# Both column groups of a pair of token tiles by seven block products, cut at 354 and 244 columns

## The chip, the cores and the metric

The kernel runs on one core of one Trainium2 chip. The metric is the device time of one execution in microseconds (us); lower is better. PE is TensorE, DVE VectorE, ACT ScalarE, POOL GpSimd, SP the engine that issues most DMAs.

## The reference

32x64 token vectors x of 1024 values pass two linear layers with low-rank experts, and x is added at the end:

```
base = x @ W.T;  logits = x @ Wr.T + 5 * one_hot(language)      # 8 experts of rank 16, top 2
y    = base + 2 * sum_e gate_e * (x @ A_e.T) @ B_e.T
out  = x + y @ Wf.T + b + 2 * sum_e softmax(y @ Wrf.T)_e * (y @ Af_e.T) @ Bm_e   # 4 experts of rank 8
```

All matrices are float32, W and Wf are 1024x1024.

## The kernel before

The kernel never forms y. It makes the fused matrix C = W.T @ [Wf.T | Wrf.T | Af.T] once (stage F, to 100 us), adds the identity to its first 1024 columns for the residual, and then multiplies the tokens by C. Every float32 product is three matmuls on rounded parts, high*high, high*low and low*high, so that one block of 128 depths is three matmuls, each with a weight load of its own. ACT rounds a value to its high part, DVE subtracts to get the low part (`low_part`, L665).

Tokens come in 16 tiles of 128 rows, taken as 8 **pairs** (`pair(j)`). In a pair the columns of C fall in two groups:

- **wide**, 2 x 384 columns (`WIDE = 3 * P`): the first two times 384 columns of z (the part of C that makes the output). The 2x2 blocks (tile 0 or 1; depths 0-511 or 512-1023; first or second 384 columns) are multiplied in the seven-product form instead of eight. P1, P2 and P4 take x itself (`of_x`), P3, P5, P6 and P7 sums of blocks of x (S1 to S4, `of_s`); the right sides are blocks of C (B11, B21, B22) or their differences T1 to T4. One product is 4 depths x 3 = 12 matmuls of 384 columns, so a pair has 84. Partial sums that two outputs share are read from PSUM in between: P1 by ACT (`r1_read`), P6, P7 and P5 by DVE (`u2_read`, `u3_read`, `r22_read`), and PE goes on accumulating in the same bank after that.
- **tail**, 428 columns (`TAIL`): the last 256 of z, 36 of the second layer's logits and projections, and 136 of the first layer's expert projections and logits (`gate_proj`). It is plain: 8 depths x 3 x 2 tiles = 48 matmuls of 428 columns per pair (`tail`), done first, since the gates hang on it.

After the tail DVE and ACT make the gates: logits, top two, exp, and the gated projections u (L958 to L981). PE turns u by two transposes (L1242), and ACT and DVE round and split it. `lora` multiplies it by c0 (three matmuls of 384 columns onto each of four banks, and of 292 for each tile's tail). Then follow the second softmax (`neg_max`, `y_exp`, v), its 32x32 transposes on DVE, and `mixed` (98 rows, 384 or 256 columns). The order of PE in a pair after the first is P1, P6, transposes, P2, lora of the tails, P7, lora, P5, lora, P4, mixed of the tails, lora, three mixed, P3, lora, mixed. The order on every engine is written by hand, and an engine's instructions run in that order. One instruction that waits holds all behind it.

The next pair's tokens are loaded by SP into `stage` when the two low parts of the pair before are made (`x_split`, L665); DVE then makes S1 to S4 (L668, L772, `add_s`), ACT rounds them, DVE splits them at the start of the next pair. Results are added up in `rows` (L995, L1026, L1035, L1043, L1046, L1049) and stored once per pair, 2 x 512 KB; the last pair stores piece by piece. Pair 0 is written apart (it overlaps the end of stage F), the loop runs pairs 1 to 7, on ACT and DVE to 6 with the last apart.

Of the kernel before, what the change touches and what calls it, by code (L numbers as in the profile page):

```python
# [5 lines left out]
def adaln_ffn_kernel(nc, part_2, part_1, part_3, part_4, tokens, gate_proj, mix_rows, language, out):  # L6

# [10 lines left out]
    F32 = mybir.dt.float32  # L18
# [7 lines left out]
    P = 128  # L26
# [17 lines left out]
    WIDE = 3 * P  # L44
    HB = part_4.shape[2]
    HTAIL = HB - WIDE
# [3 lines left out]
    Z_SECOND = P + SMALL2  # L50
    PROJ2_AT = P
    LOGIT2_AT = P + ER2
    TAIL_M = 2 * HTAIL
    PROJ_AT = TAIL_M
    LOGIT_AT = PROJ_AT + ER1
    TAIL = TAIL_M + ER1 + E1

# [13 lines left out]

    BANK_A, BANK_B, BANK_C, BANK_D, BANK_T, BANK_U, BANK_WARM = 3, 0, 1, 2, 4, 6, 7
# [6 lines left out]
    with ctx:  # L80
# [7 lines left out]
        c0_high = sb("c0_high", [P, MCOLS], F32R)  # L88
        c0_low = sb("c0_low", [P, MCOLS], F32R)
        ct_high = sb("ct_high", [P, KC, TAIL], F32R)  # L90
        ct_low = sb("ct_low", [P, KC, TAIL], F32R)
        mix = sb("mix", [MIX, D], F32R)

        c_plain = sb("c_plain", [P, 4, HALF, HB])
# [18 lines left out]
        u = sb("u", [P, 2, ER1])  # L113
        ut_high = sb("ut_high", [P, 2, P], F32R)
        ut_low = sb("ut_low", [P, 2, P], F32R)
# [5 lines left out]
        v = sb("v", [P, 2, ER2])  # L121
# [41 lines left out]
        sb("unused", [P, HALF * (2 * IN_W + 2 * ROWS_A + HB) - 4 * KC * P - 6 * HALF * WIDE - 4 * HALF * P])  # L163
# [5 lines left out]
        block_pair(T4, "t4", t_high, t_low)  # L169

# [26 lines left out]
        vt_plain = c_plain[0:ER2, C12, 0, 0:2 * P].rearrange("p (t c) -> p t c", t=2)  # L197
# [59 lines left out]

# [54 lines left out]
        def both(a, b):  # L312

            return sums[:, BANK_T:BANK_T + 2, a:b]

        def z_tail(t):

            return sums[:, BANK_T + t, 0:2 * Z_SECOND].rearrange("p (a c) -> p a c", c=Z_SECOND)[:, :, 0:P]

        def z_tails():
            return both(0, 2 * Z_SECOND).rearrange("p t (a c) -> p t a c", c=Z_SECOND)[:, :, :, 0:P]

# [37 lines left out]
        def tail_part(t, c):  # L361
            h = HALF if c in (C21, C22) else 0
            a = HTAIL if c in (C12, C22) else 0
            return t[:, h:h + HALF, a:a + HTAIL]

# [3 lines left out]
        def _(sp):  # L369
# [37 lines left out]
            def store_last(j):  # L407

                def block_out(t, a, b):
                    return sp.dma_start(out[(2 * j + t) * P:(2 * j + t + 1) * P, a:b], rows[:, t, a:b])  # L410
# [16 lines left out]
            with sp.Fori(0, PAIRS - 2) as j:  # L427
                load_pair(j + 2)
                store(j)
# [915 lines left out]
```

## Time and profile before

| | |
|---|---|
| three runs | 330.17, 330.62, 330.80 us, median 330.62 |
| the profiled execution | 331.02 us |
| its span, first to last instruction | 329.2 us |
| granted TensorE clock | 1.00 (2.4 GHz) |
| busy | PE 324.2 (98%), PEld 319.4 (97%), DVE 222.3 (68%), ACT 122.2 (37%), POOL 1.4 us |
| bytes | HBM read 18.42 MB, written 8.39 MB |

PE is the matmul row, PEld the weight loads that run beside it. Matmuls overlap (one lasts longer than the time to the start of the next), so a busy share of PE says only that it never stood idle; what a matmul costs is the distance from its start to the next start.

### The profile page before, as it was taken

How to read it: one execution, taken by the hardware profiler on the slowest of the kernel's cores; microseconds unless marked ns; L12 is line 12 of the kernel's file. 1: busy time of each engine (PE TensorE's matmuls, PEld its weight loads, DVE VectorE, ACT ScalarE, POOL GpSimd, SP SyncE). 2: the span in 40 equal slices, each digit the busy share in tenths (PEclk: the TensorE clock that was granted, in tenths of full speed). 3: DMA queues.
4: the chain of work that ended last, by engine and by line, in shares of the span. 5: the costliest groups of instructions: out<-in, count | busy, mean ns of one | idle time of the engine just before them, and what ended most of it. 6: DMA issues, size and time to landing. Idle time of an engine off the chain costs nothing.

```text
span 329.2 us, 5489 instructions
## 1 busy us (share of the span) xinstructions
PE 324.2 (98%) x2039; PEld 319.4 (97%) x2039; DVE 222.3 (68%) x492; ACT 122.2 (37%) x245; POOL 1.4 (0%) x11
## 2 busy tenths in 40 slices
PE   8999999999999999999999999999999999999996
PEld 7999999999999999999999999999999999999995
DVE  3999999998899879258447725834863582485441
ACT  3882836494247235033212513311331350332111
POOL 1000000000000000000000000000000000000000
PEclk9999999999999999999999999999999999999999
DMA  7999000000000303301600600240070033003003
GB/s 243 415 407 278 9 2 0 2 0 2 0 2 0 130 0 99 156 0 28 227 0 0 215 39 0 67 188 0 0 252 3 0 115 139 0 1 127 1 0 127
DMA packets 8188, 26.96 MB, mean 82 GB/s; under 512 B 1038, under 2 KB 2062, under 8 KB 8176
## 3 DMA queue, kind: packets, MB, share of 16 engines
q1 hardware_dynamic: 8032, 26.80, 22.8%
q8 instruction: 7, 0.11, 0.2%
q14 instruction: 5, 0.04, 0.0%
q10 hardware_dynamic: 144, 0.01, 0.0%
HBM read 18.42 MB, written 8.39 MB: 81 GB/s over the span
## 4 chain that ended last, share of the span: by engine, by line
PE 95%; DMA 2%; DVE 1%; SPq 0%; ACT 0%; issue 0%
PE sums L1063 95%; DMA in<-part 2%; PE sums L1242 1%; DVE c_plain L1019 0%; ACT a_high L459 0%; DVE rows L1026 0%; DVE rows L1049 0%; ACT y_exp L626 0%; SPq L374 0%; SPq L376 0%; DVE v L1010 0%; SPq L372 0%; DVE y_half L1007 0%; DVE neg_max L1004 0%; DVE y_scale L1008 0%
## 5 line engine op out<-in xcount | busy, mean ns | idle before, releaser
L1063 PE MATMUL sums<-b_high,a_high 128*128 128x256 f32 (+1 forms) x224 | 45.8, 288 | 0.5 <-ACT a_high L459 0.4
L1063 PE MATMUL sums<-ct_high,st_high 128*128 128x428 f32 x128 | 45.7, 357 | 0.0
L1063 PE MATMUL sums<-ct_high,st_low 128*128 128x428 f32 x128 | 45.7, 357 | 0.0
L1063 PE MATMUL sums<-ct_low,st_high 128*128 128x428 f32 x128 | 45.6, 356 | 0.0
L1063 PE MATMUL sums<-b_high,a_low 128*128 128x256 f32 (+1 forms) x224 | 45.4, 286 | 0.0
L1063 PE MATMUL sums<-b_low,a_high 128*128 128x256 f32 (+1 forms) x224 | 45.3, 285 | 0.0
L1063 PEld LDWEIGHTS sums<-b_high,a_high 128*128 128x128 f32 x224 | 34.9, 190 | 1.3 <-DVE b_high L796 0.5
L1063 PEld LDWEIGHTS sums<-b_high,a_low 128*128 128x128 f32 x224 | 34.9, 189 | 0.0
L1063 PEld LDWEIGHTS sums<-b_low,a_high 128*128 128x128 f32 x224 | 34.8, 189 | 0.0
L1063 PE MATMUL sums<-t_high,s_low 128*128 128x384 f32 x96 | 32.4, 337 | 0.0
L1063 PE MATMUL sums<-t_high,s_high 128*128 128x384 f32 x96 | 32.4, 337 | 0.0
L1063 PE MATMUL sums<-t_low,s_high 128*128 128x384 f32 x96 | 32.4, 337 | 0.0
L958 DVE TENSOR_TENSOR logits<-sums,lang_bias 128x16 f32<-128x16 f32 x8 | 1.4, 173 | 42.7 <-PE sums L1063 42.7
L609 ACT ACTIVATE pair_exp<-top 128x1 f32<-128x1 f32 x16 | 3.8, 287 | 67.8 <-DVE top_at L965 67.8
L459 ACT ACTIVATE rows<-sums 128x384 f32<-128x384 f32 (+1 forms) x24 | 12.6, 524 | 34.6 <-PE sums L1063 34.5
L1063 PEld LDWEIGHTS sums<-ct_high,st_low 128*128 128x128 f32 x128 | 24.1, 188 | 0.8
L1063 PEld LDWEIGHTS sums<-ct_low,st_high 128*128 128x128 f32 x128 | 24.1, 188 | 0.8
L1063 PEld LDWEIGHTS sums<-ct_high,st_high 128*128 128x128 f32 x128 | 24.1, 188 | 0.7
L1063 PE MATMUL sums<-c_high,st_high 128*128 128x384 f32 x64 | 22.4, 349 | 0.0
L1063 PE MATMUL sums<-c_low,st_high 128*128 128x384 f32 x64 | 21.7, 339 | 0.0
L1063 PE MATMUL sums<-c_high,st_low 128*128 128x384 f32 x64 | 21.7, 339 | 0.0
L665 DVE TENSOR_TENSOR st_low<-stage,st_high 128x1024 fp32r<-128x1024 f32 x14 | 17.1, 1225 | 5.7 <-ACT st_high L459 5.4
(132 smaller groups left out, 679.4 us busy)
## 6 DMA issues: line engine op xcount, KB each, us to landing
stage<-tokens SPq DMA_DIRECT2D x14, 512.0 KB, 3.6
out<-rows SPq DMA_DIRECT2D x14, 512.0 KB, 4.2
in<-part SPq DMA_DIRECT2D x7, 585.0 KB, 9.2
in<-part SPq DMA_DIRECT2D x4, 777.0 KB, 14.7
in<-part SPq DMA_DIRECT2D x4, 265.0 KB, 17.6
rows<-tokens SPq DMA_DIRECT2D x2, 512.0 KB, 16.2
out<-rows SPq DMA_DIRECT2D x4, 192.0 KB, 2.1
c_plain<-gate_proj SPq DMA_DIRECT2D x1, 544.0 KB, 17.1
```

What stands on the lines that cost most here:

```text
L459: return nc.scalar.activation(out_, in_, ACT.Copy)
L609: ins = nc.scalar.activation(pair_exp[:, t:t + 1], top[:, t, 0:1], ACT.Exp, bias=top[:, t, 1:2], scale=-1.0)
L665: return nc.vector.tensor_tensor(dst, src, as_f32(high), ALU.subtract)
L958: link(nc.vector.tensor_tensor(logits[:, :, :], both(LOGIT_AT, LOGIT_AT + E1), lang_bias[:, bass.ds(2 * j, 2), :], ALU.add))
L1063: return nc.tensor.matmul(out_, lhs, rhs, start=start, stop=stop, skip_group_check=True)
L1242: last = nc.tensor.transpose(ut_psum[:, t, :], u[:, t, :], ident[:, :])
```

## The change

Columns are regrouped. Halves of C are now the two natural halves of z (512 columns each) with the 18 columns of the second layer behind each. The wide group is the first 354 columns of each half (`WIDE = 354`). Of each half the rest, 158 of z and 18, together with half of the 136 gate columns (68), is a **narrow** group of 244 columns (`NARROW`). Pairs 0 and 1 do the narrow group as the tail was done, by 48 matmuls of 2 x 244 = 488 columns. From pair 2 on it goes by seven block products too (`narrow_products`): 84 matmuls of 244 columns into banks 4, 5 and 6. Four more right sides (`tn_high`, `tn_low`) are made in pair 1, for which the gate columns are loaded once more by four DMAs, 272 bytes a run. The partial sums are read into a new tile `narrow`, by ACT (two reads of 244 columns) and DVE (five additions); after mixed, DVE adds the narrow sums to z's last columns (632 elements; ACT copied 512 before), and a new small addition makes `sec`. S sums, their roundings and splits move to other places in the order.

```diff
-    WIDE = 3 * P
+    WIDE = 354
+    GH = (ER1 + E1) // 2
+    NARROW = GH + HTAIL
-    BANK_A, BANK_B, BANK_C, BANK_D, BANK_T, BANK_U, BANK_WARM = 3, 0, 1, 2, 4, 6, 7
+    BANK_A, BANK_B, BANK_C, BANK_D, BANK_T, BANK_U, BANK_WARM = 3, 0, 1, 2, 4, 7, 7
+    BANK_NA, BANK_NB, BANK_NC = 4, 5, 6
...
 # SP
+            sp.wait_ge(cw_split, 3)
+            sp.wait_ge(t_split, 4)
+            for c in (C11, C12, C22, C21):
+                ...
+                sp.dma_start(c_plain[:, c, :, GATE_AT:WIDE], gate_proj[:, k:k + HALF, a:a + GH])\
+                    .then_inc(gate_again, 16)
...
 # ACT, pair(j)
+                if steady:
+                    act.wait_ge(p1n_done, j - 1)
+                    copy(narrow[:, 1, 0, :], narrow_bank(BANK_NA)).then_inc(r1n_read, 1)
+                    act.wait_ge(p2n_done, j - 1)
+                    copy(narrow[:, 0, 0, :], narrow_bank(BANK_NA)).then_inc(n11_out, 1)
-                act.wait_ge(tails_done, j + 1)
-                copy(rows[:, :, 2 * WIDE:D]..., z_tails()).then_inc(tails_out, 1)
...
 # DVE, pair(j)
-                    for n in (S2, S1, S3, S4):
-                        split_s(j, n)
+                    split_s(j, S1)
+                    split_s(j, S4)
+                if second:
+                    dve.wait_ge(gate_again, 64)
+                    make_tn(C11, C12, C11, t1n_made)
+                    make_tn(C12, C22, C12, t3n_made)
+                    split_tn(T1)
+                    make_tn(C11, C22, C11, t2n_made)
+                    next_s(S1)
+                    split_tn(T3)
...
+                if steady:
+                    link(add_sums(sec_halves, tails(SEC_AT, NARROW), narrow[:, :, :, SEC_AT:NARROW]))
+                else:
+                    link(nc.vector.tensor_copy(sec_halves, tails(SEC_AT, NARROW)))
...
 # PE
+            def narrow_product(n, a_high, a_low, a_at, b_high, b_low, fresh):
+                for k in range(HALF):
+                    for kind in (HH, HL, LH):
+                        lhs = (a_high, a_high, a_low)[kind]
+                        rhs = (b_high, b_low, b_high)[kind]
+                        last = mm(narrow_bank(n), lhs[:, a_at[0], a_at[1] + k, :], rhs[:, k, :],
+                                  start=fresh and k == 0 and kind == HH, stop=k == HALF - 1 and kind == LH)
+                return last
...
             pair(0, first=True)
-            with pe_loop(1, PAIRS) as j:
+            pair(1, second=True)
+            with pe_loop(2, PAIRS) as j:
                 pair(j)
```

PE at the start of a pair in the loop, up to the first wide product. L1063, now L1258, is the helper that issues every matmul; c11 is B11, ct holds the tail's columns of C. Before:

```order
L1218 REGISTER_ALU [waits tails_out]
L1063 MATMUL sums<-ct_high,st_high 128x428 [waits x_split_0]
L1063 MATMUL sums<-ct_low,st_high 128x428
L1063 MATMUL sums<-ct_high,st_low 128x428
...
L1063 MATMUL sums<-ct_high,st_high 128x428 [waits x_split_1]
...
L1063 MATMUL sums<-c11_high,st_high 128x384 [waits a_out]
```

Now, of the products P1, P6, P2, P7, P5, P4 and P3 the first matmul each:

```order
L1258 MATMUL sums<-ct_high,st_high 128x244 [waits x_split_0]
...
L1258 MATMUL sums<-ct_high,s_high 128x244 [waits s_split]
...
L1258 MATMUL sums<-ct_high,st_high 128x244 [waits r1n_read]
...
L1442 REGISTER_ALU [waits u2n_read]
L1258 MATMUL sums<-t_narrow,s_high 128x244 [waits s_split]
...
L1258 MATMUL sums<-t_narrow,s_high 128x244 [waits s_split]
...
L1258 MATMUL sums<-t_narrow,st_high 128x244 [waits u3n_read,x_split_1,tn_split]
...
L1258 MATMUL sums<-ct_high,s_high 128x244 [waits r22n_read,s_split]
...
L1258 MATMUL sums<-c11_high,st_high 128x354 [waits a_out]
```

Beside the waits for operands there are now four for reads of the banks (r1n_read by ACT; u2n_read, u3n_read, r22n_read by DVE), each of the result of the last product but one.

DVE at the start of a pair in the loop, up to the logits. Before:

```order
L665 TENSOR_TENSOR s_low<-s_plain,s_high 128x512 [waits s_rounded]
L756 REGISTER_ALU
L665 TENSOR_TENSOR s_low<-s_plain,s_high 128x512 [waits s_rounded]
L957 REGISTER_ALU
L958 ISA [waits narrow_ready]
L958 TENSOR_TENSOR logits<-sums,lang_bias 128x16
```

Now, after the splits of S1 and S4:

```order
L1039 TENSOR_TENSOR narrow<-sums,narrow 128x244 [waits p6n_done,r1n_read]
L1039 TENSOR_TENSOR narrow<-sums,narrow 128x244 [waits p7n_done]
L866 ISA
L867 ISA [waits s_split]
L869 TENSOR_TENSOR s_plain<-stage 128x512 [waits x_here_1,x_here_0]
L1039 TENSOR_TENSOR narrow<-sums,narrow 128x244 [waits p5n_done,u3n_read]
L871 REGISTER_ALU
L765 TENSOR_TENSOR s_plain<-s_plain,stage 128x512 [waits s1_made]
L1039 TENSOR_TENSOR narrow<-sums,narrow 128x244 [waits p4n_done]
L765 TENSOR_TENSOR s_plain<-stage 128x512
L1039 TENSOR_TENSOR narrow<-sums,narrow 128x244 [waits p3n_done,u2n_read]
```

Three S sums of the next pair (s_plain) stand now between the additions, and the first of them waits for the next pair's tokens (x_here). At the end of a pair the low part of the next pair's second tile (st_low) has moved from before L1043's addition to behind that of L1046.

## Rows read from the trace of the kernel before

**Rows 1.** The page: busy time of each engine, and the granted clock in 40 slices

```profile
PE 324.2 (98%) x2039; PEld 319.4 (97%) x2039; DVE 222.3 (68%) x492; ACT 122.2 (37%) x245; POOL 1.4 (0%) x11
...
PEclk9999999999999999999999999999999999999999
```

**Rows 2.** The chain that ended last: start us, us, engine, what, count

```profile
119.22 0.18 DVE neg_max L1004
...
121.91 0.57 DVE rows L1026
...
199.12 27.92 PE sums L1063 x156
227.04 0.22 PE sums L1242 x2
```

**Rows 3.** Engines in a steady pair: stretch, us, busy us of each (instructions), PEclk, DMA

```profile
213.30:241.44 28.14, 28.14 (x160) 27.80 (x160) 15.82 (x44) 7.86 (x19) 0.00 (x0) 1.00 0.21 75
```

**Rows 4.** Timeline of PE: start us, us, instruction; places where the form changes

```profile
60.28 0.28 PE L1063 MATMUL sums<-b_high,bt_high 128*128 128x256 f32 x1
...
60.64 0.29 PE L1063 MATMUL sums<-b_high,bt_high 128*128 128x274 f32 x1
...
61.02 0.41 PE L1063 MATMUL sums<-b_high,a_high 128*128 128x256 f32 x2
...
201.09 0.30 PE L1063 MATMUL sums<-c_high,ut_high 128*128 128x292 f32 x1
...
201.89 0.34 PE L1063 MATMUL sums<-t_high,s_high 128*128 128x384 f32 x1
...
213.30 0.35 PE L1063 MATMUL sums<-ct_high,st_high 128*128 128x428 f32 x1
...
222.64 0.34 PE L1063 MATMUL sums<-c_high,st_high 128*128 128x384 f32 x1
...
226.88 0.38 PE L1242 MATMUL sums<-ident,u 128*128 128x128 f32 x2
227.02 0.42 PE L1063 MATMUL sums<-c_high,st_high 128*128 128x384 f32 x1
227.28 0.34 PE L1063 MATMUL sums<-c_low,st_high 128*128 128x384 f32 x1
...
232.64 0.34 PE L1063 MATMUL sums<-t_high,s_high 128*128 128x384 f32 x1
...
234.72 0.34 PE L1063 MATMUL sums<-c_high,ut_high 128*128 128x384 f32 x1
```

**Rows 5.** Groups by form, weight loads: xcount, busy us, mean ns of one

```profile
L1063 PEld LDWEIGHTS sums<-ct_high,st_high 128*128 128x128 f32 x128 | 24.1, 188 | 0.7
```

**Rows 6.** Groups by form, DVE: what the added instructions are priced by

```profile
L665 DVE TENSOR_TENSOR s_low<-s_plain,s_high 128x512 fp32r<-128x512 f32 x28 | 17.5, 686 | 1.7 <-ACT s_high L459 1.6
L665 DVE TENSOR_TENSOR ut_low<-sums,ut_high 128x256 fp32r<-128x256 f32 x8 | 3.4, 424 | 0.7 <-ACT ut_high L459 0.7
L747 DVE TENSOR_TENSOR c_plain<-sums,c_plain 128x548 f32<-128x548 f32 x6 | 4.3, 718 | 0.0
L665 DVE TENSOR_TENSOR st_low<-stage,st_high 128x1024 fp32r<-128x1024 f32 x14 | 17.1, 1225 | 5.7 <-ACT st_high L459 5.4
```

**Rows 7.** Timeline of DVE and ACT in a steady pair (last bracket: idle before, releaser)

```profile
212.44 0.55 DVE L1043 TENSOR_TENSOR rows<-sums,rows 128x384 f32<-128x384 f32 x1
212.91 0.55 DVE L1046 TENSOR_TENSOR rows<-sums,rows 128x384 f32<-128x384 f32 x1
...
222.96 0.17 DVE L958 TENSOR_TENSOR logits<-sums,lang_bias 128x16 f32<-128x16 f32 x1 [6.08 <-PE sums L1063]
...
225.02 0.49 ACT L459 ACTIVATE rows<-sums 128x384 f32<-128x384 f32 x1 [0.47 <-PE sums L1063]
...
226.11 0.34 DVE L981 SCALAR_TENSOR_TENSOR u<-sums,pair_scale,gates 128x128 f32<-128x128 f32 x1
```

**Rows 8.** The tile stage: its DMAs' time to landing

```profile
DMA to landing us min/median/max: 3.4/3.6/5.1
```

**Rows 9.** Timeline of PE in pair 0: the wait before P4

```profile
121.96 0.34 PE L1063 MATMUL sums<-c_high,ut_low 128*128 128x384 f32 x1
...
122.61 0.41 PE L1063 MATMUL sums<-t_high,st_high 128*128 128x384 f32 x1 [0.31 <-DVE rows L1026]
```

More of the change, by code:

```diff
@@ L636, in pair @@
                 copy(vt[0:ER2, :, :], vt_plain[0:ER2, :, :]).then_inc(v_rounded, 1)
-                if not first:
-                    act.wait_ge(stored[0], 16 * j)
-                act.wait_ge(tails_done, j + 1)
-                copy(rows[:, :, 2 * WIDE:D].rearrange("p t (a c) -> p t a c", c=P), z_tails()).then_inc(tails_out, 1)
+                if not first and not last:
+                    round_next(j + 1, S3, p7_done)
                 if not last:
@@ L645, in pair @@
                     round_x(j + 1, 1)
+                if not first:
+                    act.wait_ge(stored[0], 16 * j)
                 act.wait_ge(a_done, j + 1)
-                copy(rows[:, 0, 0:WIDE], bank(BANK_A)).then_inc(a_out, 1)
+                copy(rows[:, 0, wide_at(0)], bank(BANK_A)).then_inc(a_out, 1)
+                if first:
+                    round_next(j + 1, S2, p6_done)
+                    round_next(j + 1, S3, p7_done)
+                if not last:
+                    round_next(j + 1, S1, p5_done)
             pair(0, first=True)
-            with act.Fori(1, PAIRS - 1) as j:
+            pair(1, second=True)
+            with act.Fori(2, PAIRS - 1) as j:
                 pair(j)
@@ L911, in _ @@
             split_tail(C12)
-            dve.wait_ge(ident_added, 2)
+            dve.wait_ge(ident_added, 1)
             add_out(Q_P7, C22, 0, C22)
@@ L938, in _, with make_tn, split_tn, add_sums @@
             split_t(T3, C12)
+            def make_tn(dst, a, b, made):
+                minus(narrow_of(dst), narrow_of(a), narrow_of(b)).then_inc(made, 1)
+            def split_tn(n):
+                dve.wait_ge(tn_rounded, TN_ORDER.index(n) + 1)
+                low_part(tn_low[n], narrow_of(C12 if n == T3 else C11), tn_high[n]).then_inc(tn_split, 1)
+            def add_sums(dst, n, onto):
+                return nc.vector.tensor_tensor(dst, n, onto, ALU.add)
             STEPS = 14
             BLOCK = 32
-            def pair(j, first=False, last=False):
+            def pair(j, first=False, second=False, last=False):
+                steady = not first and not second
                 base = STEPS * j + VEC_START
@@ L1030, in pair @@
                 if not last:
                     split_x(j + 1, 0)
[L1033 to L1039 removed]
+                if first:
+                    add_r22()
+                    for n in MADE:
+                        next_s(n)
@@ new lines, in pair @@
+                if second:
+                    split_s(j + 1, S2)
+                if steady and not last:
+                    split_s(j + 1, S3)
+                dve.wait_ge(tails_done, j + 1)
+                if steady:
+                    add_sums(rows_tail, tails(GH, SEC_AT), narrow[:, :, :, GH:SEC_AT]).then_inc(tails_out, 1)
+                else:
+                    nc.vector.tensor_copy(rows_tail, tails(GH, SEC_AT)).then_inc(tails_out, 1)
+                if second:
+                    split_s(j + 1, S3)
@@ L1055, in _ @@
             pair(0, first=True)
-            with dve.Fori(1, PAIRS - 1) as j:
+            pair(1, second=True)
+            with dve.Fori(2, PAIRS - 1) as j:
                 pair(j)
```

471 lines of the change are left out of this document (314 added, 157 removed).

## The prediction

> **What bounds the kernel now.** I read the page's busy shares first: PE 98%, weight loads 97%, DVE 68%, ACT 37%, clock at the upper level (2.4 GHz) in all 40 slices [rows 1]. Then the chain that ended last: from 123 us on it is nothing but matmuls, in steps of 28.14 us (27.92 and 0.22) with no other engine in between [rows 2]. The steady pairs are thus pure matmul time: in one, PE is busy for all 28.14 us and DVE for 15.82 [rows 3]. So the change is worth what it does to the matmuls' own distances, less any wait it brings in. The distances come from the timeline, by dividing the stretch between two changes of form by the matmuls in it [rows 4]:
>
> - 128 columns: two transposes and one wide matmul take 227.28 - 226.88 = 0.40 us; less 0.175 for the wide one leaves 0.11 each
> - 256: (60.64 - 60.28) / 3 = 120 ns
> - 274: (61.02 - 60.64) / 3 = 127 ns
> - 292: (201.89 - 201.09) / 6 = 133.3 ns
> - 384: (226.88 - 222.64) / 24 = 176.7 ns, and (234.72 - 232.64) / 12 = 173.3 ns; I take 175.5
> - 428: (222.64 - 213.30) / 48 = 194.6 ns
>
> A slice of columns costs about 0.46 ns per column at the top, and about 0.38 between 256 and 292.
>
> **The change, part by part.** Measured in columns it gives almost nothing on the narrow side: 48 x 428 = 20,544 before, 84 x 244 = 20,496 after. The eighth product that is saved pays for the 30 columns by which each wide matmul shrinks.
>
> *Wide, every pair.* 84 matmuls go from 384 to 354 columns. Between 292 and 384 a column costs (175.5 - 133.3) / 92 = 0.459 ns, so 30 columns are 13.8 ns and a pair saves 84 x 13.8 = 1.16 us.
>
> *Narrow, pairs 2 to 7.* 48 x 194.6 = 9.34 us go. What 244 columns cost no row shows; the nearest is 256 at 120 ns. From below, 244 in proportion to the 384 row (0.457 ns each) is 111.5 ns; from above, no gain on 256 at all, 120 ns, if the weight load sets the pace. I take the line through 256 and 274, 120 - 12 x 0.39 = 115.3 ns, as the nearest rows lie on it: 84 x 115.3 = 9.69 us, so +0.35 us (bounds +0.03 and +0.74).
>
> A rule speaks against this part. Each matmul here has a weight load of 128 columns, and the two transposes, which move only 128 columns, still stand 0.11 us apart [rows 4]: there the load, not the stream, sets the pace. The Trainium skill (page "TensorE: Matmul & The Clock Gate", section "LDWEIGHTS (loading the stationary operand)") gives a load as columns / 1.2, 107 ns for 128, which the 0.11 bears out, and under its "Back-to-back issue gap" N / 2.4 + 2.5 ns for the stream, 104 ns for 244 columns. By the page a 244-column matmul would be held by its load at 107 ns. With its own figures for 354, 384 and 428 as well (150, 162.5, 180.8) a pair would gain an estimated 1.05 - 0.31 = 0.74 us, close to what I get; but 384 columns measure 175.5 and not 162.5, so the sum goes by the rows.
>
> *Lora and mixed.* 12 lora and 4 mixed matmuls lose 30 columns (-0.22 us), 6 grow from 292 to 352 (+0.165), 2 from 256 to 316 (+0.045): nothing.
>
> **A steady pair** comes to -1.16 + 0.35 = -0.81 us, 27.33 after 28.14; six of them -4.9 us (bounds: 1.13 each, -6.8; 0.42 each, -2.5).
>
> *Pairs 0 and 1* have the longer plain tail: 60 columns more at 194.6 / 428 are 27.3 ns, times 48 is +1.31 us; the wide side gives 1.16 back. +0.15 each, +0.3.
>
> *New waits in the narrow products.* P2, P7, P4 and P3 each wait for a read of a bank, and one other product (12 x 115 ns = 1.38 us) covers it. A reader starts about 0.3 us after the next product's first matmul (logits at 222.96 after 222.64 [rows 4, 7]), lasts 0.42 us (256 columns [rows 6]; ACT about the same, 0.49 for 384 [rows 7]), and PE goes on some 0.14 us after it (L1026 from 121.91 for 0.57, P4 at 122.61 [rows 2, 9]): 0.86 of 1.38 us. For P3 DVE also makes S1 (0.69 us by the 512-column row [rows 6]) between P7's and P5's addition; from the end of P7 that is 0.3 + 0.42 + 0.69 = 1.4, P5 ends at 1.38, its addition at 2.1 and P3 is due at 2.76. Hidden, with half a microsecond to spare.
>
> *The next pair's tokens.* S1 waits for x_here. The second low part of x is now made later, behind the additions to D's and B's rows. Counted from P4's end, DVE has before the load can be issued: the first low part (1.23 less 0.08, as a following instruction overlaps it), a split of S3 (0.6), the new 632-column addition (548 columns take 718 ns [rows 6], so 0.8), two additions of 354 columns (0.47 from start to start at 384 [rows 7], so 0.9) and the second low part, 1.2: 4.6 us, where PE needs 3.9 to the pair's end (lora, mixed, P3 by its 12 x 162 ns, lora, mixed). The load is issued up to 0.8 us into the next pair. It lands after 3.6, at worst 5.1 us [rows 8], so at 4.4 to 5.9. S1 is wanted at 6.2 (P7's end at 5.5, then 0.3 and 0.42) and stalls PE only if it starts after 7.0. Hidden; this is the thinnest cover.
>
> *Gates.* They start with P3's last addition, 0.5 us later than before, then take 226.45 - 222.96 = 3.5 us [rows 7]; the transposes now stand behind P1, P6 and P2, 84 / 7 x 3 x 162 ns = 5.8 us. Hidden, 1.8 to spare.
>
> *DVE in a steady pair:* five additions of 0.42, one of 0.81 and one of about 0.25 are +3.2 us on 15.8, 19 of 27.3 us. ACT gets two reads of 0.4 and loses one copy. Neither becomes the bound.
>
> *Pair 0* is where a wait stands already. After u's product for the tails, the chain goes through neg_max, exp, v and its transposes to L1026, and P4 waits for it: 122.61 where 122.14 was due, 0.47 us [rows 2, 9]. The change puts the copy `sec` and a link in front of neg_max (about 0.38 us), and PE arrives at P4 0.25 us earlier, since P7, lora and lora have shrunk: +0.6 us (0.2 to 1.0).
>
> *Pair 1* makes the four narrow right sides: 976 elements each, four subtractions and four splits, near the 1024-column row [rows 6] 1.17 us each, 9.4 us on top of 16: DVE is busy for 26 of 28.3 us. Four of them hide in the tail (10.7 us); two of them and two S sums stand before neg_max, after which the same chain as in pair 0 has P7, P5 and two lora as cover, 4.8 us for about 4.3. +0.2 us (0 to 0.8). The four gate DMAs are issued in pair 0 and wanted some 12 us later, more than twice the longest landing of the 512 KB loads [rows 8]; SP has them ahead of pair 2's load, which isn't due yet. Nothing.
>
> *Stage F and the end:* the same matmuls in F, the same last store. Nothing, within 0.3.
>
> **The sum:** -4.9 + 0.3 + 0.6 + 0.2 = **-3.8 us**. The profiled execution took 331.02 (span 329.2), so 327.2 by it; it lay 0.4 above the median, and against the median of 330.62 I predict **326.8 us**.
>
> **Rivals.**
>
> 1. *The load sets the pace below 256 columns.* A narrow matmul costs 120 ns like the 256-column one. For it: loads are 97% busy [rows 1], and from 292 to 256 the price falls more slowly than above. Against: 274 to 256 still falls by 7 ns. Then a pair gains 0.42, six 2.5, less 1.1: -1.4, **329.2 us**. Chance 0.25. The skill's load rule points this way, though to a lower floor.
> 2. *Slower by the token load.* S1 stands in DVE's queue ahead of the addition that frees P3's bank. If the load, which now shares the DMA engines with the two 512 KB stores, lets S1 start at 8.15 us instead of 6.2, P3 starts 1.15 us late in six pairs: +6.9 - 3.8 = +3.1, **333.7 us**. It costs the whole gain from 7.65 us on. Against: the load is issued before the stores. Chance 0.08.
> 3. *Small waits in each steady pair*, 0.5 to 0.6 us in all, as DVE is fuller and reads stand close before PE's waits: -3.8 + 3.4, **330.2 us**. Against: each cover above has 0.5 us. Chance 0.09.
> 4. *Loads no longer hide.* A narrow matmul is paced by the whole 188 ns of its load [rows 5]: 84 x 188 = 15.8 us, a pair is 5.3 us longer, +32 - 3.8 + 4.9 = +33, **364 us**. Against: 256 columns run at 120, far under 188. Chance 0.03.
>
> **How the numbers follow.** My forecast has 0.55. About 0.2% (0.66 us) is what a measurement of this kernel can tell from no change. Faster is the forecast, rival 1 and a little of rival 3: 0.82. Same is most of rival 3: 0.07. Slower is rivals 2 and 4: 0.11. The forecast's ends: -6.8 + 0.3 + 0.2 is 324.3; -2.5 + 0.3 + 1.8 is 330.2, which takes in rival 1 and half of rival 3. The range is 324.3 to 330.3.
>
> **What would show it.** A steady pair of 27.3 us instead of 28.14; the seven narrow products 9.7 us from first to last, 115 ns a matmul; wide ones at 162; in pair 0 about 1.1 us before P4; no PE idle after pair 1. Wrong if 244 columns take 120 ns or more, if a steady pair holds an idle PE before P3 or P2, or if S1 on DVE waits for a DMA.

## The result, and the profile after

The changed kernel takes **328.89 us** (median of 6 runs, 328.4 to 329.51), the kernel before on the same chip 330.86 (6 runs, 330.17 to 331.62): a ratio of 0.9941, 95% interval 0.9924 to 0.9959. That is 2.0 us faster where 3.8 were forecast; the direction came as forecast and the time lies in the stated range, but about half of the gain is missing. The profiled execution took 328.5 us with a span of 326.1. The span is the time from the first to the last instruction of the profile; what the execution takes more than that is called the time **beyond the span** here.

The page of the changed kernel, answering [rows 1]:

```profile
PE 319.6 (98%) x2255; PEld 314.3 (96%) x2255; DVE 246.9 (76%) x543; ACT 126.9 (39%) x251; POOL 1.4 (0%) x11
```

The engines in a steady pair, in pair 0 and in pair 1 (columns as in [rows 3], which the first line answers):

```profile
212.21:239.53 27.32, 27.32 (x195) 27.30 (x195) 18.41 (x51) 8.19 (x20) 0.00 (x0) 1.00 0.22 76
99.49:128.90 29.41, 28.58 (x160) 26.68 (x159) 24.31 (x51) 14.14 (x25) 0.00 (x0) 1.00 0.19 55
128.90:157.55 28.65, 28.65 (x159) 26.72 (x159) 26.37 (x57) 11.46 (x22) 0.00 (x0) 1.00 0.24 84
```

A steady pair is 27.32 us of PE without a gap, against 28.14 before. The timeline of PE where the form changes, and the wait of pair 0, to be read as [rows 4, 9]:

```profile
122.99 0.40 PE L1258 MATMUL sums<-t_high,st_high 128*128 128x354 f32 x1 [0.83 <-DVE rows L1039]
...
212.21 0.28 PE L1258 MATMUL sums<-ct_high,st_high 128*128 128x244 f32 x1
...
221.76 0.33 PE L1258 MATMUL sums<-c_high,st_high 128*128 128x354 f32 x1
...
225.64 0.32 PE L1258 MATMUL sums<-c_high,st_high 128*128 128x354 f32 x1
```

84 narrow matmuls take 221.76 - 212.21 = 9.55 us, 113.7 ns each; 24 wide ones 3.88 us, 161.7 ns each. So far this is the forecast. The first matmul of pair 0's tails and the last matmul of the program, of the kernel before and then of the changed one:

```profile
100.16 0.35 PE L1063 MATMUL sums<-ct_high,st_high 128*128 128x428 f32 x1
...
325.68 0.33 PE L1063 MATMUL sums<-mix,vt 98*128 98x384 f32 x1
```

```profile
321.33 0.33 PE L1258 MATMUL sums<-mix,vt 98*128 98x354 f32 x1
```

The changed kernel's pair 0 starts at 99.49 (the window above). From there to the last matmul are 225.5 us before and 221.8 after: **-3.7 us**. The loss is behind the last matmul. Timeline of VectorE and of the stores there, after:

```profile
318.58 0.82 DVE L1039 TENSOR_TENSOR rows<-sums,narrow 128x632 f32<-128x632 f32 x1 [1.35 <-PE sums L1258]
319.31 0.95 DVE L1039 TENSOR_TENSOR rows<-sums,rows 128x354 f32<-128x354 f32 x2
321.69 0.53 DVE L1039 TENSOR_TENSOR rows<-sums,rows 128x354 f32<-128x354 f32 x1 [1.43 <-PE sums L1258]
```

```profile
319.42 1.30 SPq L467 DMA_DIRECT2D out<-rows  x2
320.77 2.10 SPq L464 DMA_DIRECT2D out<-rows  x4
```

The last matmul starts at 321.33, the last store is issued at 322.40, SP, which waits for it, goes on ("sees" it) at 325.34, and the span ends at 326.1: 4.78 us of end. Before, the last matmul started at 325.68, the store was issued at 326.64 and seen at 328.50: 3.56 us. And the time beyond the span is 1.81 us in 17 runs of the kernel before, but 2.41 on average in 6 of the changed one (1.93 to 2.87). DMA of both kernels from 318 to 335 us in 40 slices, the kernel before first, then the changed one:

```profile
DMA  0000000000000477999600660000000000000000
```

```profile
DMA  0000005699999920000000200000000000000000
...
q8 instruction: 1, 0.02, 0.5%
q14 instruction: 2, 0.02, 0.4%
```

Before, the DMA engines have gone idle when the last store comes; after, there is no gap. The profile lists reads of the program's own instructions among the DMA packets, on queues of their own. In this window the kernel before has one, of 8 KB on q14; the changed kernel has two of 8 KB on q14 and one of 16 KB on q8. The reads of q8 are called TensorE's below, since they moved with the length of TensorE's program alone (experiments 8, 10 and 11).

Below, times are medians, "end" is from the start of the last matmul to the end of the span in the profile, "beyond" the time less the span.

### The profile page after: what moved, and what is told of

It reads as the page before. It is cut to its first block, busy times and chain, and to the rows that moved or that the text cites. A ratio compares the mean times of both kernels' runs of the same rounds, so it can differ in the third digit from the quotient of the medians.

```text
span 326.1 us, 6003 instructions
## 1 busy us (share of the span) xinstructions
PE 319.6 (98%) x2255; PEld 314.3 (96%) x2255; DVE 246.9 (76%) x543; ACT 126.9 (39%) x251; POOL 1.4 (0%) x11
## 4 chain that ended last, share of the span: by engine, by line
PE 96%; DMA 1%; DVE 1%; ACT 0%; SPq 0%; issue 0%
PE sums L1258 95%; DMA in<-part 1%; PE sums L1500 1%; DVE rows L1039 0%; DVE vt_plain L1202 0%; ACT y_exp L718 0%; SPq L428 0%; DVE a_low L762 0%; DVE v L1193 0%; ACT a_high L526 0%; SPq L426 0%; DVE sec L1184 0%; DVE y_half L1190 0%; DVE y_scale L1191 0%; DVE neg_max L1185 0%
## 5 line engine op out<-in xcount | busy, mean ns | idle before, releaser
L1258 PE MATMUL sums<-b_high,a_high 128*128 128x256 f32 (+1 forms) x224 | 45.7, 288 | 0.1
L1258 PE MATMUL sums<-b_high,a_low 128*128 128x256 f32 (+1 forms) x224 | 45.3, 286 | 0.0
L1258 PE MATMUL sums<-b_low,a_high 128*128 128x256 f32 (+1 forms) x224 | 45.3, 285 | 0.0
L1258 PEld LDWEIGHTS sums<-b_high,a_high 128*128 128x128 f32 x224 | 34.9, 190 | 0.7 <-DVE a_low L762 0.4
L1258 PEld LDWEIGHTS sums<-b_high,a_low 128*128 128x128 f32 x224 | 34.8, 189 | 0.0
L1258 PEld LDWEIGHTS sums<-b_low,a_high 128*128 128x128 f32 x224 | 34.8, 189 | 0.0
L1258 PE MATMUL sums<-t_high,s_high 128*128 128x354 f32 x96 | 31.6, 329 | 0.0
L1039 DVE TENSOR_TENSOR rows<-sums,rows 128x354 f32<-128x354 f32 x48 | 24.4, 522 | 9.3 <-PE sums L1258 9.0
L1258 PE MATMUL sums<-t_low,s_high 128*128 128x354 f32 x96 | 31.1, 324 | 0.0
L1258 PE MATMUL sums<-t_high,s_low 128*128 128x354 f32 x96 | 31.1, 324 | 0.0
L1258 PE MATMUL sums<-ct_high,st_high 128*128 128x244 f32 (+1 forms) x80 | 25.6, 320 | 0.0
L1258 PE MATMUL sums<-ct_low,st_high 128*128 128x244 f32 (+1 forms) x80 | 25.5, 319 | 0.0
L1258 PE MATMUL sums<-ct_high,st_low 128*128 128x244 f32 (+1 forms) x80 | 25.5, 319 | 0.0
L1258 PE MATMUL sums<-c_high,st_high 128*128 128x354 f32 x64 | 21.0, 328 | 0.0
L1258 PE MATMUL sums<-c_low,st_high 128*128 128x354 f32 x64 | 20.8, 325 | 0.0
L1258 PE MATMUL sums<-c_high,st_low 128*128 128x354 f32 x64 | 20.7, 324 | 0.0
L1258 PEld LDWEIGHTS sums<-t_low,s_high 128*128 128x128 f32 x96 | 18.2, 189 | 0.0
```

The costliest lines, as they stand in the source:

```text
L1039: return nc.vector.tensor_tensor(dst, n, onto, ALU.add)
L1258: return nc.tensor.matmul(out_, lhs, rhs, start=start, stop=stop, skip_group_check=True)
```

## Experiment 1: is it the longer program?

The kernel before with pair 1 written out, as in the change (`pair(1)` ahead of each loop, loops from 2, on PE, DVE and ACT).

> The kernel before with pair 1 written out on PE, ACT and DVE and the loops from pair 2: the same instructions are executed, the program is longer, as in the change. Theory A (the 0.2 to 1.1 us by which the changed kernel's time exceeds its span more than before's 1.8 us come from the longer program): time minus span goes from 1.8 to 2.3 us or more, the time up by about 0.5 us, ratio 1.0015. Rival B (they have another cause or are scatter): time and span as before within 0.3 us.

Measured: 330.80 us (11 runs) against 330.75, ratio 1.0001 (0.9992 to 1.001); 1.90 us beyond. Pair 1 written out costs nothing that these runs can tell, at most 0.3 us by the interval. That does not clear the program's length: this kernel has neither TensorE's read behind the span nor VectorE's among the last stores, and experiments 8 to 11 show that where the reads fall is what counts.

## Experiment 2: the last stores in four pieces

```
-                tail_out(0).then_inc(stored[0], 16)
-                tail_out(1).then_inc(stored[1], 16)
-                block_out(0, wide_at(0)).then_inc(stored[0], 16)
+                block_out(0, half(0)).then_inc(stored[0], 16)
...
-                block_out(0, wide_at(1)).then_inc(stored[0], 16)
+                block_out(0, half(1)).then_inc(stored[0], 16)
```

> The changed kernel; the last pair stores four pieces of 512 columns (2048 bytes a row) instead of six of 354 and of 2 x 158. Theory A (the six pieces, two of them of 632-byte runs and 0.6 us to issue, make the last store land 2.9 us after its issue instead of 1.9): from the last matmul to the end of the span 4.8 us become about 4.0, time -0.8 us against the changed kernel. Rival B (the end is bound by bytes or by the size of the last piece, which grows from 177 to 256 KB): no gain, -0.2 to +0.4 us.

Measured: 328.26 us (6 runs), 0.6 below the change, though the two intervals overlap (ratio 0.9915 to 0.9939, the change's 0.9924 to 0.9959). Its profile is of the slowest of the six runs: span 327.3, where the other five have 325.3 to 326.0 and the change 326.1 to 327.0. It has the last store issued at 323.40 and seen only at 326.60, end 4.85 us. Each store is moved by sixteen DMA engines, and each of them adds to the store's semaphore when it is done (the trace has sixteen packets of 4 bytes and sixteen updates for each store). By the trace's packets and semaphore updates fifteen of the sixteen had landed at 325.41; the last one has 8 KB of instructions between its packets, from 325.23 to 325.54, and lands at 326.58. That is 1.2 us for one read, and without it this end would be about 3.7 us (an estimate: 4.85 less 1.17). So the stores' shape may be worth about 0.5 us, but this run does not show it clear of the noise.

## Experiment 3: the wait of pair 0

`add_u3()` before VectorE's four transposes in pairs 0 and 1, not behind them.

> The changed kernel; in pairs 0 and 1 DVE adds P7's result (u3) before the four 32x32 transposes, not behind them. Theory A (PE's waits before P4 in pair 0, 1.0 us, and pair 1, 0.25 us, hang on that order): pair 0's wait falls to 0.2 us, pair 1's to none, time -0.8 to -1.1 us against the changed kernel. Rival B (vt is then late and PE waits the same before mixed, or before the next pair's tokens): less than 0.3 us.

Measured: 329.14 us (5 runs), nothing gained, as rival B had it. The waits of PE in pair 0, by the waits view:

```profile
PE sums L1258 <- DVE rows L1230: 0.4, 1, 0.4
PE sums L1258 <- DVE rows L1039: 0.2, 1, 0.2
```

The wait before P4 (0.8 in the same view of the change) has shrunk to 0.2, and a new one of 0.4 stands before pair 1's tails, for the copy of the tails, which is queued behind four sums. Pair 0 takes 29.62 us (29.41). The time moved along VectorE's queue.

## Experiment 4: the same columns without the narrow products

The changed kernel with 354/244 columns, but every pair with the plain tail of 488 columns.

> The changed kernel's columns (354 and 244), but no narrow products: pairs 2 to 7 do the narrow group as pair 1 does, by 48 matmuls of 488 columns, and the narrow right sides are not made. Theory A (the gain of the change is all in the matmuls of the six pairs, 84 x 113.6 ns for 48 x 221.9): a steady pair takes 28.3 us instead of 27.32, time +5.9 us or a little less against the changed kernel, about 334.5. Rival B (the narrow products bring waits that eat part of it): a steady pair under 28.1, total under 333.5.

Measured: 334.82 us (5 runs), 5.9 above the change; 334.5 was expected. Its steady pair (columns as above) is 0.17 us longer than the 28.3 expected:

```profile
213.67:242.14 28.47, 28.47 (x160) 26.74 (x159) 16.67 (x46) 7.57 (x17) 0.00 (x0) 1.00 0.21 74
```

The narrow products are worth 28.47 - 27.32 = 1.15 us a pair, 6.9 in six. Only 5.9 show in the time, mainly because this kernel's end is 3.93 us, 0.85 less than the change's: it has no VectorE read among the last stores (experiments 5 and 6). Shrinking the wide columns without them is a loss: 0.33 us more than the 28.14 of before.

## Experiments 5 and 6: one store at the end

Five of the last pair's six stores are left out, in the kernel before (b_one) and in the changed one (e_one).

> The kernel before, with five of its last pair's six stores left out (the last one, of the 128 x 384 block that the last product makes, stays; the outputs of the other five blocks of that pair are not written). It is the control for the next run. In the kernel before, the profile shows the DMA engines idle before the last store is issued, and that store lands 1.86 us after its issue; from the start of the last matmul to the end of the span are 3.56 us. Theory 'backlog' (the end of the changed kernel is longer because its six stores queue up behind one another): here nothing was queued, so the end stays at 3.4 to 3.6 us. Theory 'engines' (the end is set by what the engines do after their last instruction): also 3.4 to 3.6 us. Time 330.3 to 330.9 us.

> The changed kernel with the same five stores left out (the last store, 128 x 354, stays; the outputs of the other five blocks of the last pair are not written). Its end, from the start of the last matmul to the end of the span, is 4.78 us in the profile, 1.2 us more than before, and its last store lands 2.94 us after its issue. Theory 'backlog': without the five stores in front of it the last one lands 1.8 to 1.9 us after its issue, and the end falls to 3.5 to 3.7 us, the kernel before's; the span falls by 1.1 us. Theory 'engines' (instruction fetches and the engines' own finish make the end, whatever is stored): the end stays at 4.5 to 4.8 us. The time beyond the span stays at 2.4 us by both.

Measured: before, 330.61 us (one run), end 3.27 us. Changed: 328.95 us (one run), end 4.61 us; **"backlog" fell** as the main cause, as the queue was empty and the end still long. The one store in the DMA view (window 322 to 327), first of the kernel before, then of the changed one:

```profile
out<-rows SPq DMA_DIRECT2D x1, 192.0 KB, 1.9
```

```profile
q14 instruction: 2, 0.02, 0.8%
...
out<-rows SPq DMA_DIRECT2D x1, 177.0 KB, 2.9
```

A smaller store takes 1.0 us longer. The trace's packets and semaphore updates part this in two. In the changed kernel 15 DMA engines are done with it at 324.38 us; the sixteenth has 8 KB of instructions to read in between, from 324.40 for 309 ns, starts its last piece at 324.71 and writes its semaphore at 324.77. The fifteen updates have landed at 325.31, the sixteenth lands at 325.75, and SP sees it at 325.77: **the read costs 0.44 us**. The other 0.6 us are not the read's. On the engines that nothing disturbs, 0.88 us pass between an engine's last packet and the landing of its update (median of the sixteen), where b_one has 0.33. The last store, where it has 354 columns, shows 0.62 to 0.93 in every profile, among them two without any such read: 0.75 in experiment 4 and 0.78 in e_st (below). Stores of 384 and of 512 columns show 0.33 to 0.42 throughout. So this part goes with the 354-column store. It is larger for tile 0, whose store is the last one, than for tile 1 (0.41 and 0.41 in e_steps), and why such a store lands later stays open.

The read comes 1.1 us after VectorE's closing instruction (323.30 us). A read on q14 stands 1.0 to 1.4 us behind it in the change (323.7 there), in experiments 2, 3, 7 and 8 and in e_fill below, and there is none among the last stores in the kernel before, in experiments 1 and 4, whose VectorE has less code, or in e_steps, where VectorE's program alone is shorter. In the seven profiles with the read VectorE's closing instruction starts 0.7 us after the one before it, in the eleven without 0.01 to 0.11. That the read is VectorE's is inferred from this.

## Experiment 7: how low can a narrow matmul go?

`rhs[:, k, 0:194]` in the narrow products: 50 of 244 columns of each are left out.

> The changed kernel with the narrow products of the six steady pairs cut from 244 to 194 columns (50 columns of each are left out, so these outputs are wrong there); everything else stays. It asks whether a weight load sets a floor under the distance of two matmuls. Measured so far: 113.6 ns for 244 columns, 162.4 for 354. Theory 'columns' (the line through these two, 0.44 ns a column): 91 to 94 ns for 194 columns, a steady pair 84 x 21 ns = 1.8 us shorter (25.5 us), the kernel 10 us shorter, near 318.5. Theory 'load' (the Trainium skill, page TensorE: Matmul & The Clock Gate, section LDWEIGHTS: 128 columns at 1.2 a nanosecond): 107 ns, a pair 0.55 us shorter (26.8 us), the kernel 3.3 us shorter, 325.5. A third outcome: if VectorE or the wait for the gate becomes late in the shorter stretch, TensorE waits and the pair is longer than 84 times the distance says.

Measured: 327.35 us (one run). Its steady pair, and the first narrow and the first wide matmul in PE's timeline:

```profile
212.34:239.50 27.16, 27.16 (x196) 27.13 (x196) 18.42 (x51) 8.23 (x20) 0.00 (x0) 1.00 0.23 78
```

```profile
212.34 0.26 PE L1258 MATMUL sums<-ct_high,st_high 128*128 128x194 f32 x1
...
221.70 0.35 PE L1258 MATMUL sums<-c_high,st_high 128*128 128x354 f32 x1
```

9.36 us for 84: **111.4 ns for 194 columns**, 113.7 for 244. 50 columns fewer are worth 2 ns, with nothing waited for, where "columns" wanted 91 to 94 ns. There is a floor, and the changed kernel stands 2 ns above it. It is what the transposes hinted at [rows 4]. The Trainium skill (page "TensorE: Matmul & The Clock Gate", section "LDWEIGHTS (loading the stationary operand)") gives a load as its columns / 1.2, an estimated 107 ns for 128 columns; the measured floor is 4 ns above it. So "load" came out in kind, but its figures were low: a pair of 26.8 us was expected and 27.16 measured, 325.5 us in all and 327.35 measured. That the floor is the load's own time is argued from this nearness; no run here changes the size of the load.

## Experiment 8: TensorE's code longer at its end

```
             with pe_loop(2, PAIRS) as j:
                 pair(j)
+            for _ in range(120):
+                pe.wait_ge(cleared, 1)
```

> The changed kernel with 120 waits on a semaphore that has long been reached, at the end of TensorE's program behind its last matmul, where TensorE is 4 us ahead of the end of the span. It asks about the 0.6 us more beyond the span (time less span: 1.8 us for the kernel before, 2.4 for the changed one). The profiles that show more than 2.3 us there all hold a read of 16 KB by TensorE's instruction queue 1.3 to 1.9 us after the span's end; those with 1.8 us hold none. Theory 'read' (the time is that of this read, which TensorE asks for when it comes near the end of its code): the added instructions make it ask earlier, under the stores, and the time beyond the span falls to 1.8 us, the time to 328.3. Theory 'other' (the read goes with the end of the program, wherever TensorE's code stands): 2.3 to 2.5 us, time 328.7 to 329.1. If the waits cost more than 33 ns each, TensorE ends last and the span grows.

Measured: 328.97 us (4 runs), where theory "read" expected 328.3. Beyond is 1.80 to 1.85 us in all four, as it said, but the span grew to 327.15 in the median, from 326.5. TensorE is done before SP here (its closing instruction starts at 325.67, SP's at 326.43), so the waits themselves do not make the end. TensorE's read has moved from 1.3 us past the end of the span to 320.05 us, among the stores. The first line of the stores, after 1.30 us in the change:

```profile
319.32 2.06 SPq L467 DMA_DIRECT2D out<-rows  x2
```

The issue of the second one alone took 1.36 us in place of 0.60, the stores after it come later by as much, and the end is 5.46 us, 0.7 longer than the change's. So the read cost 0.6 to 0.7 us in either place.

## Experiments 9 to 11: both reads out of the way

```
-            STEPS = 14
+            STEPS = 10
```

takes 16 empty instructions from VectorE's program (e_steps);

```
+            def fill(first):
+                for _ in range(20 if first else 0):
+                    pe.wait_ge(cleared, 1)
```

is called behind six products of `pair` and gives TensorE ten instructions more at each in pair 0 (e_fill); e_both has both.

> The changed kernel with 16 empty instructions fewer in VectorE's program: each of the four pairs written out (first, second, the loop's, the last) counts a semaphore up to 14 where 10 are needed; now it counts to 10. Nothing is computed differently. It asks what makes the end 1.2 us longer. In every run of the changed kind VectorE's queue reads 8 KB of instructions about 1.0 us after VectorE's last instruction, on one of the DMA engines that carry the last stores; in the kernel before, and in the one with a pair written out, there is no such read, and the run with a single store still had the long end and the read. Theory 'VectorE's read': with 1 KB less of code the read is not reached before the end, the last store is seen 2.0 to 2.3 us after its issue (after 2.9), the end falls from 4.8 to 3.9 to 4.2 us, the time to 328.0 to 328.4. Theory 'stores': the read stays or makes no difference, end 4.6 to 4.9 us, time 328.7 to 329.1. The time beyond the span stays at 2.4 by both.

> The changed kernel with 60 more instructions in TensorE's program (120 waits on a semaphore long reached), put into pair 0 in six groups between products, where TensorE's sequencer runs over 2 us ahead of its matmuls and should hide 1 us of them at a time. It asks about the time beyond the span, which the run with the same 60 instructions behind the last matmul brought from 2.4 to 1.84 us, but whose span grew by as much, since the 16 KB read then fell among the last stores and one store's issue took 1359 ns in place of 604. Theory 'place of the read': with the code moved by 4 KB the read comes inside the loop, away from both, the time beyond the span is 1.75 to 1.9 us and the span that of the changed kernel (326.4 to 326.7 in the median), the time 328.1 to 328.5. Rival: the read again falls within the last stores (a read by TensorE's queue between 316 and 326 us): the span grows, time 328.8 to 329.1. If the waits are not hidden, pair 0 is longer than 29.4 us by up to 6 us.

> The changed kernel with both: 16 empty instructions fewer on VectorE and 60 more on TensorE in pair 0. If the 1.2 us of the end and the 0.6 us beyond the span are two reads of instructions that come at the wrong moment, the two gains add: end 3.9 to 4.2 us, 1.8 us beyond the span, time 327.2 to 327.8 us. If they are one effect, or neither, the time is that of the better of the two runs before.

Measured, beside 330.80 for the kernel before (9 runs):

| run | us (median, runs) | end | beyond, mean | reads at the end |
|---|---|---|---|---|
| change | 328.89 (6) | 4.78 | 2.41 | VectorE's, TensorE's |
| e_steps | 328.58 (5) | 4.27 | 2.45 | TensorE's |
| e_fill | 328.19 (5) | 5.08 | 1.86 | VectorE's |
| e_both | 327.60 (4) | 4.38 | 1.81 | neither |

e_both has a ratio of 0.9901 (0.9886 to 0.9916) to the kernel before. By the profile's end and the mean beyond, e_steps takes away 0.5 us and e_fill 0.55. Alone they are 0.3 and 0.7 us below the change in the medians, with intervals (0.9914 to 0.9941 and 0.9908 to 0.9935) that overlap the change's; together they are 1.3 below, and there the intervals lie apart. So the sum is shown clear of the noise, and the two add to within 0.3 us; each one's share rests on the profiles and on the means beyond. No computing was saved and none moved, only empty instructions. The 60 extra instructions are free where the sequencer is ahead (pair 0 stays 29.41). DMA from 325.5 to 329.5 us, the instruction queues' lines of the change:

```profile
q8 instruction: 1, 0.02, 2.2%
q14 instruction: 1, 0.01, 0.9%
```

and of e_fill, where TensorE's queue q8 reads nothing there:

```profile
q14 instruction: 1, 0.01, 0.5%
```

Whether q8 reads there agrees with the time beyond the span in every profile of this study: 2.4 to 2.9 us with the read, 1.75 to 2.0 without; in one run (e_last2, below), 2.09 with it. The agreement is closer than that: in all ten profiles with the read, the execution's time is the moment at which the read ends, counted from the first instruction, less 0.24 or 0.25 us (the change: read from 327.36 for 1.38 us, so to 328.74, and 328.50 measured). The read thus sets the end of the execution wherever it comes, and in e_last2 it is cheap because it starts early. Two of the change's own six runs have only 1.93 and 2.0 beyond, so the read does not come, or not late, in every run.

## Experiments 12 and 13: the rest of the end, and of pair 0

e_last is e_both with the tail product ahead of the three low-rank ones in steady pairs too (`mixed_tails(j)` before `lora(BANK_B, 1, 0)`) and the last pair stored in five pieces; e_best adds experiment 3's move and puts two of pair 0's four S sums behind the copy of the tails:

```
+                block_out(0, slice(HZ + WIDE, D)).then_inc(stored[0], 16)
...
+                block_out(0, slice(0, HZ)).then_inc(stored[0], 16)
...
+                block_out(1, slice(HZ, D)).then_inc(stored[1], 16)
...
+                block_out(1, slice(0, HZ)).then_inc(stored[1], 16)
```

> The kernel of the last run (both instruction reads out of the way) with its last stores made differently: the product that completes the tail columns comes before the three low-rank products of the fourth bank in every pair from the third on (0.5 us earlier), and the last pair is stored in five pieces (the right tail of tile 0, three whole halves of 512 columns, the last wide block) in place of six, so that no piece has runs of 632 bytes in two places a row. It asks what is left of the longer end: 4.38 us in that run's profile, 3.56 in the kernel before. Theory 'backlog' (what is left is the stores queued before the last one: its store is seen 2.5 us after its issue, 1.9 before): the last store is seen 1.9 to 2.2 us after its issue, the end falls to 3.7 to 4.0 us, the time from 327.6 to 327.0 to 327.3 us. Rival: the DMA engines move the same 1.05 MB in the same time after the same last matmul, end 4.3 to 4.5 us, time 327.4 to 327.8.

> The kernel of the last line with the order of VectorE's work changed in pairs 0 and 1: the addition that the second-last product waits for comes before the four transposes (as in the run above, whose pair 0 was no shorter because VectorE was late later in the pair), and in pair 0 two of the four sums of the next pair's blocks come behind the copy of the tails, for which TensorE waited 0.55 us there. Theory 'order' (pair 0's extra 0.7 us is VectorE doing things in the wrong order): the wait before pair 1 is gone, pair 0 takes 28.9 to 29.2 us in place of 29.4, pair 1 28.4 in place of 28.65, time 0.4 to 0.7 us below the other kernel's. Theory 'bound' (VectorE has more work in pair 0 than TensorE): pair 0 stays at 29.4 to 29.6 us, because the sums that were moved back are then late themselves, and the time is within 0.2 us of the other kernel's.

Measured: e_last 328.34 us (5 runs), where both theories had 327.8 or less; end 4.05, but 2.58 beyond: TensorE's read is back, at 327.6 us. e_best 328.26 (6 runs). Its pairs 0 and 1:

```profile
100.57:129.62 29.05, 28.82 (x160) 26.59 (x159) 23.41 (x50) 12.78 (x22) 0.00 (x0) 1.00 0.20 56
129.62:158.53 28.91, 28.69 (x160) 26.76 (x159) 26.33 (x56) 12.85 (x24) 0.00 (x0) 1.00 0.23 79
```

Together 57.96 us, 58.06 in the change: what pair 0 gained, pair 1 gave back. The waits view of the two pairs:

```profile
PE sums L1509 <- DVE u L1130: 0.2, 1, 0.2
PE sums L1261 <- DVE rows L1039: 0.2, 1, 0.2
```

The first is new and stands in pair 1, where the transposes wait for u: VectorE starts that pair with the work moved back from pair 0 and comes to the logits 11.39 us into it, 10.85 in the change. "Bound" is right for the two pairs taken together, as VectorE is busy for 26.3 of pair 1's 28.9 us and has no room for what pair 0 leaves it.

## Experiments 14 to 16: what brings the read back?

e_st is e_both with the five-piece store alone, e_ord with the order of TensorE alone, e_last2 is e_last with 30 filling instructions in place of 60.

> The kernel with both instruction reads away (327.6 us) with the five-piece store of the last pair alone; TensorE's, VectorE's and ScalarE's programs are the same as there. In the run that had both this store and the earlier tail product, the end was 4.05 us (4.38 without them) but TensorE's 16 KB read after the end was back, with 2.5 us beyond the span. Theory 'TensorE's order brings the read back': here there is none, 1.75 to 1.9 us beyond the span; the end is 4.1 to 4.4 us, the time 327.2 to 327.6. Rival 'the stores bring it back' (an end in which the queues fall silent earlier): 2.4 to 2.6 us beyond the span, the time 328.0 to 328.4.

> The same kernel (327.6 us) with the tail product ahead of the three low-rank products alone; the code is as long, and the six stores are as in the change. Theory 'TensorE's order brings the read back': 2.4 to 2.6 us beyond the span, the time 328.0 to 328.4. Rival 'the stores': 1.75 to 1.9 us beyond the span, the first store 0.5 us earlier, the end 4.0 to 4.3 us, the time 327.2 to 327.6.

> The kernel with both (store in five pieces, tail product earlier; 328.34 us, with the read back), with 30 instructions fewer in TensorE's program of pair 0 (30 added in place of 60). Theory 'place in the code' (whether the read comes is a matter of where TensorE's code ends against the blocks it is read in): with 2 KB less the read may be gone, then 1.75 to 1.9 us beyond the span and 327.0 to 327.5 us; if it stays, 328.1 to 328.5 us, and length alone does not decide it.

Measured, beside 330.71 us: e_st 327.67 (4 runs), end 3.94, beyond 1.91, no read. e_ord 327.88 (6 runs), end 3.90, beyond 1.89 to 2.84, the read in its profile. e_last2 327.56 (4 runs), end 3.99, beyond 2.02, a read at 326.9 us, 1.0 past the span. TensorE's order brings it back, the stores don't; and both the place of the code and something that changes from run to run have a part in it, since e_ord has runs of both kinds. By what rule it comes stays open. e_both, e_st and e_last2 are equal within 0.1 us and the fastest, 1.2 to 1.3 us under the change and 3.0 to 3.2 under the kernel before.

## Why the prediction was wrong in its size

- **Wide matmuls**: -13.8 ns each was forecast, 161.7 measured. Right.
- **Narrow products**: 115.3 ns forecast, 113.7 measured. Right, and inside the bounds. The 1.6 ns are mostly rounding in my line: taken in nanoseconds over all of stage F, 256 columns stand 119.2 ns apart and 274 columns 127.2, and the line through these gives 113.9 for 244. Experiment 7 shows that a floor exists below, at 111.4 ns, so the line would have failed at 194 columns; the choice of 244 lies just above the corner, which I did not know. Rival 1 had a floor, but put it at 120 ns, 8.6 too high. That the measured time, 328.89, lies 0.3 us from that rival's 329.2 is a coincidence: its loss was to be in the steady pairs, and they show none.
- **A steady pair**: 27.33 forecast, 27.32 measured; no wait in any of six. Rivals 2, 3 and 4 are refuted. P3's and the token load's cover held for PE (the loads landed after 3.4 to 4.5 us, [rows 8] had up to 5.1). One of my signs of being wrong did show, harmlessly: in pair 2 S1 on DVE waits 0.18 us for its load (at 163.79 us), and PE does not stop.
- **Pair 0**: +0.15 and +0.6 forecast, 28.72 to 29.41 = +0.69 measured; PE's wait before P4 is 0.83 us. **Pair 1**: +0.15 and +0.2 forecast, +0.51 measured (28.14 to 28.65), 0.15 more.
- Up to the last matmul the sum was thus -3.8 against -3.7 measured.
- **"Stage F and the end: the same matmuls in F, the same last store. Nothing, within 0.3."** This is the step that failed. The end measured +1.2 us. 0.5 of it is VectorE's instruction read on a DMA engine of the last store (4.78 to 4.27 in e_steps; 0.44 by the packets of e_one). Nor was it "the same last store": of the 0.8 us that e_both keeps, 0.4 lie between the last packet and SP's seeing it (0.77 us, 0.35 before), 0.3 in the store's packets, which end 1.77 us after its issue (1.50 before) as it queues behind others, and 0.1 in a later issue. In e_st and e_ord, where the stores before it have room, the packets are as fast as before (1.49 and 1.53) and only the first part is left, with ends of 3.94 and 3.90; but their times are not below e_both's, so what the queue costs in time stays open. So does why the 354-column store is seen later. Stage F differs from profile to profile (99.4 to 100.6 us to pair 0, in kernels with the same code there too) and says nothing.
- **A term that was not in the sum**: the time beyond the span, taken as unchanged when I went from the span to the time, grew by 0.6 us with TensorE's 16 KB read. Experiments 8, 10 and 11 show it by its removal, and the time follows the read's end to 0.01 us in ten profiles.

So -3.7, +1.2, +0.6 is -1.9, the measured -2.0. With both reads out of the way the same change gives -3.2.

## What to carry to other kernels

Where matmuls with a fresh 128-column weight load each are the bound, count matmuls and not columns once a group is narrow: here 194 columns cost 111.4 ns and 244 cost 113.7. Where a kernel's code grows, look at the instruction queues' reads in the last microseconds: one that fell on the last stores, or just behind the end, cost 0.4 to 0.7 us here (1.2 in one profile), and 16 empty instructions fewer on VectorE or 60 more on TensorE, at a place where it was ahead, moved it; a change of TensorE's order brought one back (e_ord). And a wait on an engine that is itself nearly full was not removed by moving its instructions; in both trials here it came back later, in the same pair or the next.

## What the runs showed of the hardware that was not expected

- The distance of two matmuls that each load 128 columns of weights: 111.4 ns at 194 columns, 113.7 at 244, 119.2 at 256, 161.7 at 354. From 244 to 256 a column costs 0.46 ns, as it does above; from 194 to 244 it costs 0.05.
- 60 satisfied waits in TensorE's program cost about 0.1 us each behind the last matmul (105 ns from start to start), and nothing in groups of ten between products.
- A 16 KB instruction read by TensorE behind the span (0.93 to 1.38 us long) set the time of the execution: its end less 0.24 or 0.25 us, in ten profiles of ten.
- An 8 KB instruction read of 309 ns on one of 16 DMA engines delayed that engine's part of the last store by 0.44 us (e_one) and by 1.2 us (e_half).
- The last store of 354 columns landed 0.62 to 0.93 us (median of the engines) after its last packets, stores of 384 and 512 columns 0.33 to 0.42, with the read or without it.
